# One product with C for two neighbouring units in the recurrent stage of a decoder kernel

## The reference, cut to what matters

```python
def _selective_scan(u, dt, A, Bm, Cm, Dp):
    dA = jnp.exp(dt[..., None] * A)
    dBu = (dt * u)[..., None] * Bm[:, :, None, :]
    def step(h, inp):
        dA_t, dBu_t, C_t = inp
        h = dA_t * h + dBu_t                       # state of 16 per channel
        y = jnp.einsum('ben,bn->be', h, C_t)
        return (h, y)
    ...
    return y + u * Dp

def _mamba(x, in_w, cw, cb, xw, dtw, dtb, A_log, Dp, ow):
    u, z = jnp.split(x @ in_w, 2, axis=-1)         # 512 channels each
    u = jax.nn.silu(causal convolution of u with 4 taps + cb)
    dbl = u @ xw                                   # 64 of dt, 16 of B, 16 of C
    dt = jax.nn.softplus(dbl[..., :64] @ dtw + dtb)
    y = _selective_scan(u, dt, -jnp.exp(A_log), Bm, Cm, Dp)
    return (y * jax.nn.silu(z)) @ ow

for i in range(4):
    x = x + _mamba(layer_norm(x), ...)
```

## Time and profile before

| | |
|---|---|
| median of 3 runs | 4773.03 us |
| profiled execution | 4812.17 us, its span 4810.5 us |
| recurrent stage, first to last scan | 70.95 to 2069 us of the span |
| one of its 16 segments, mean | 125 us |
| VectorE busy over the span | 66%, in the recurrent stage 94% |
| scans: count, mean | 1024, 1251 ns |
| products with C: count, mean | 1024, 675 ns |
| decays: count, mean | 1024, 689 ns |
| drives: count, mean | 1024, 1274 ns |

### The profile page before, as it was taken

One profiled execution on the slowest core, in us unless ns is written; L12 is line 12 of the kernel. 1 busy time (PEld: TensorE's weight loads), 2 busy tenths in 40 slices (PEclk: granted clock), 3 DMA queues, 4 the chain that ended last, 5 costly groups with the idle time before them and its releaser, 6 DMA issues. The chain is left out here.

```text
span 4810.5 us, 50784 instructions
## 1 busy us (share of the span) xinstructions
PE 4110.7 (85%) x16032; PEld 2276.1 (47%) x16032; DVE 3197.0 (66%) x5216; ACT 2001.7 (42%) x3534; POOL 2265.1 (47%) x1928
## 2 busy tenths in 40 slices
PE   7888888888998888759858887999968999966998
PEld 2333333333333333224432336888833444655898
DVE  4999999999999999954466645444445554155433
ACT  5666566656565656432234451111112444222100
POOL 6888888888888888820021112444330111000320
PEclk9999999999999999979768898999977999988899
DMA  4555544554455544510062201000061320000000
GB/s 121 133 134 147 136 139 134 139 140 141 134 136 146 140 133 134 143 43 0 0 122 33 40 11 57 14 26 26 1 155 48 53 52 10 9 16 0 27 20 29
DMA packets 288996, 375.34 MB, mean 78 GB/s; under 512 B 100481, under 2 KB 131516, under 8 KB 288508
## 3 DMA queue, kind: packets, MB, share of 16 engines
q1 hardware_dynamic: 288764, 372.57, 30.4%
HBM read 343.80 MB, written 26.21 MB: 77 GB/s over the span
## 5 line engine op out<-in xcount | busy, mean ns | idle before, releaser
L521 POOL TENSOR_TENSOR arena<-arena 128x512 f32<-128x512 f32 x1024 | 1284.3, 1274 | 260.3 <-DVE psum L764 254.6
L764 DVE TENSOR_TENSOR_SCAN psum<-psum,arena 128x512 f32<-128x512 f32 x1024 | 1280.6, 1251 | 78.7 <-ACT psum L670 78.0
L871 PE MATMUL psum<-arena,base 128*128 128x512 f32 x2048 | 1083.9, 631 | 262.5 <-DVE arena L739 261.5
L670 ACT ACTIVATE psum<-arena 128x512 f32<-128x512 f32 x1024 | 699.5, 689 | 271.5 <-DVE arena L739 252.6
L871 PEld LDWEIGHTS psum<-arena,base 128*128 128x128 f32 x2048 | 348.5, 192 | 921.9 <-DVE arena L739 745.0
L739 DVE TENSOR_TENSOR arena<-psum,arena 128x512 f32<-128x512 f32 x1024 | 691.3, 675 | 0.0
L283 POOL TENSOR_TENSOR rounded<-arena,rounded 128x512 fp32r<-128x512 f32 (+2 forms) x181 | 315.9, 1751 | 791.8 <-DVE rounded L279 791.8
L289 PE MATMUL psum<-rounded 128*128 128x256 f32 (+1 forms) x1728 | 561.6, 325 | 33.1 <-DVE arena L1689 16.2
L290 PE MATMUL psum<-rounded 128*128 128x256 f32 (+1 forms) x1728 | 561.0, 325 | 0.0
L291 PE MATMUL psum<-rounded 128*128 128x256 f32 (+1 forms) x1728 | 560.3, 324 | 0.0
L1158 DVE TENSOR_REDUCE arena<-psum 128x1 f32<-128x512 f32 (+3 forms) x768 | 403.2, 555 | 199.6 <-PE psum L1221 139.1
(11 more groups left out here) (287 smaller groups left out, 5171.7 us busy)
## 6 DMA issues: line engine op xcount, KB each, us to landing
arena<-mb_bc_rows SPq DMA_DIRECT2D x512, 512.0 KB, 4.8
arena<-L_ffn_w SPq DMA_DIRECT2D x34, 512.0 KB, 4.4
arena<-f_parts SPq DMA_DIRECT2D x96, 128.0 KB, 6.5
arena<-l_parts SPq DMA_DIRECT2D x96, 128.0 KB, 6.4
l_v<-arena SPq DMA_DIRECT2D x16, 512.0 KB, 3.6
arena<-l_v SPq DMA_DIRECT2D x32, 256.0 KB, 4.4
f_parts<-arena SPq DMA_DIRECT2D x24, 256.0 KB, 2.4
l_parts<-arena SPq DMA_DIRECT2D x24, 256.0 KB, 2.4
```

The lines of the kernel that those rows point to most:

```text
L521: eng.tensor_tensor(drive[:, u % RD, :], dtu[:, g % 2, m, :], bc_sb[:, v % RB, 0, :], ALU.mult)\
L670: eng.activation(ps[:, DECAY + u % ND, :], dt[:, g % 2, m, :], ACT.Exp, scale=a_neg[:, g // 4 % 2, m, n:n + 1]).then_inc(decay_ready, 1)
L764: eng.tensor_tensor_scan(state(u), state(u), drive[:, u % RD, :], first, ALU.mult, ALU.add).then_inc(scanned, 1)
L871: eng.matmul(ps[:, Y + u % 2, :], sh.ident, hc[:, u % RW, :], start=False, stop=n == NS - 1).then_inc(added_up, 1)
```

## The change

The product with C is made for two neighbouring units (an even u and u+1) at once. The two units' states lie in neighbouring PSUM banks, their products in neighbouring places of the ring, and they share the C row, which is read twice through a broadcast. The pair product stands behind the scan of u+2, so that one scan of the next pair lies between the pair's last scan and its product. Its signal counts two units at once. The two gates that stood ahead of the products of p = 0 and 1 (and 32 and 33) now both stand ahead of the pair product of p = 0 (and 32). The lines from there on move by two or three.

```diff
-        def weigh(u):
-            eng.wait_ge(scanned, u + 1)
+        def weigh_pair(u):
+            eng.wait_ge(scanned, u + 2)
             if u >= RW:
-                eng.wait_ge(added_up, u - RW + 1)
-            eng.tensor_tensor(hc[:, u % RW, :], state(u), bc_sb[:, u // 2 % RB, 1, :], ALU.mult).then_inc(weighted, 1)
+                eng.wait_ge(added_up, u - RW + 2)
+            at, r = DECAY + u % ND, u % RW
+            c_rows = bc_sb[:, u // 2 % RB, 1, :].unsqueeze(1).to_broadcast([P, 2, BANK])
+            eng.tensor_tensor(hc[:, r:r + 2, :], ps[:, at:at + 2, :], c_rows, ALU.mult).then_inc(weighted, 2)
 
-        def gate_before(u):
+        def gates_before(u):
             at = u - HALF
-            if at >= 0 and u % HALF < 2:
-                gate(at // UNITS, at % UNITS // HALF, u % HALF)
+            if at >= 0 and u % HALF == 0:
+                for q in range(2):
+                    gate(at // UNITS, at % UNITS // HALF, q)
...
             eng.tensor_tensor_scan(state(u), state(u), drive[:, u % RD, :], first,
                                    ALU.mult, ALU.add).then_inc(scanned, 1)
-            if u:
-                if u >= HALF + 1 and (u - 1) % HALF < 2:
-                    gate_before(u - 1)
-                weigh(u - 1)
+            if u and u % 2 == 0:
+                gates_before(u - 2)
+                weigh_pair(u - 2)
...
-        weigh(SEGS * UNITS - 1)
+        weigh_pair(SEGS * UNITS - 2)
```

## The result

The changed kernel took 5089.44 us (median; 5088.41 to 5093.23), against 4777.48 us of the kernel before beside it: 1.0657 times as long, interval 1.0627 to 1.0687, 312 us more. The prediction said 5008, range 4900 to 5100, slower with a chance of 0.94. The profiled execution has a span of 5091.5 us. Times and ratios are those of runs in the chip's fast state; a run of split (5690.97 us) and one of the kernel before (10143.09) are in the slow one and not counted.

What follows compares the result with a forecast made beforehand. The prediction took VectorE's ordered list plus its waits to bound the recurrent stage. Added wait of 255 us less 20 us saved work made +235, giving 5008 us, range 4900 to 5100.

Steps and rivals of the forecast that it cites:

- forecast as sized: Whole kernel: added waits less saved work make +235 us, time between 4930 and 5060; chance 0.73.
- the clock's rival: TensorE's clock falls behind new idle pieces, delaying three chains per segment by 1.7 us each: 77 us more, 5085; chance 0.10.
- scans 4, 6: At p = 3 and 5, ScalarE's normalized rows make the next even decay 2.2 us late each: +4.4 per segment.
- additions at 8, 10: VectorE's additions of the last segment's output wait for TensorE's output products: 1.36 and 1.14 us, +1.8 per segment.
- scans 27, 37: At p = 26 and 36, ScalarE's table loads and Silu delay decays: 2.55 and 2.5 us, +4.3 per segment.
- both gates at 34: Gates ahead of the pair product wait for the sum over unit 31, among two convolutions: 4.5 us, +2.5 per segment.
- scan 44: At p = 43, the rows of dt, B and C make decay 44 late: +2.4 us per segment, nothing before.
- The saved instruction: 1024 products of 512 columns become 512 of 1024, saving 0.04 us a pair: 20 us (25 lost to 56 saved).
- The rival of the larger saving: Each pair saves 0.11 us, 56 us in all, and the lead suffices: faster, 4717; chance 0.03.
- The lost lead: Decay ring of four banks: even units keep 1.04 us of lead, before 3.35; added waits 255 us.
- sum per segment: Added waits: 18.0 us in an even segment, 15.6 in an odd one, mean 17, times 15 segment transitions: 255 us.
- Covering for each other: Rival: a wait at one place lets TensorE and ScalarE catch up, taking off 85 us: 4923; chance 0.11.

Runs made afterwards that it cites:

- split: The changed kernel with its pair product written as two products of 512 columns, same place in VectorE's list, each with its own signal: 4994.46 us, 1.044.
- jobs: The changed kernel with three of ScalarE's tasks for the next segment one place later (p = 4, 6 and 44): 4975.72 us, 1.0416.
- near: The changed kernel with the pair product directly behind its own second scan, no scan of the next pair in between: 4900.09 us, 1.0245.
- warm: The changed kernel with three dummy TensorE products of 512 columns at each of p = 3, 35 and 61: 5071.11 us, 1.0606.
- after: The changed kernel itself, with the pair product of 1024 columns, against the kernel before: 5089.44 us, 1.0657.

## Why the prediction came out as it did

The direction and the mechanism were right, and the time lay near the upper end of the range: +235 forecast, +312 measured. It lies outside the forecast as sized (4930 to 5060, chance 0.73) and 4 us from the time of the clock's rival (5085, chance 0.10); the range holds it because it was drawn to take that rival in. Delays in one even segment, in steps, from the starts in its timeline:

| place | forecast | measured after |
|---|---|---|
| scans 4, 6 | 2.2, 2.2 | 2.2, 2.2 |
| additions at 8, 10 | 1.36, 1.14 | 3.1, 1.2 |
| scans 13, 17 | as before, 1.85 | 1.7, 1.7 |
| scans 27, 37 | 2.55, 2.5 | 2.7, 2.5 |
| both gates at 34 | 4.5 | 4.5 |
| scan 44 | 2.4 | 4.6 |
| scan 56 | 0.84 | 0.83 |
| scan 63 | 3.6 | 3.65 |
| second gate at 2 | not priced | 0.8 |

- **The saved instruction** was sized at 0.04 us a pair by the step; it is 0.08 in the even segments (3.36 against 3.44) and some 0.06 in the odd ones. Over the stage 18 us of work went by the recorded waits, forecast 20; it is some 30 if each wait is counted from the step, as there are 123 waits more that each read 0.09 too short. The rival of the larger saving needed 0.11 a pair and a lead that suffices, and the waits refute it. By the Trainium skill, "VectorE: DVE Perf Modes" (The TRN2 errata), the saving would be 80 us, an estimate; its advice of larger tiles holds here in direction and not in size (18 to 30 us).
- **The lost lead**: ten of the twelve prices for an even segment hold within 0.2 us. (Two figures of the prediction are slightly off as worked out there: 5.2 against 0.6 + 3.40 makes the second addition 1.2 late and not 1.14, and the chain of the earlier trace rows is 1.5 times its window and not nearly twice.) jobs and near show the mechanism by itself, and split shows that it is the place in the list.
- **The mis-sized term** is the sum per segment. 17 us were forecast and some 22 measured (323 / 15): 302, 76 and 57 us of waits for decays, gates and additions, where the prediction looked for 280, 65 and 35. The two places of the table that are far off, the first addition and scan 44, and the second gate at p = 2, are those where TensorE worked behind an idle piece at a lower clock: 1.7, 2.2 and 0.8 us in the even segment, some 3 in the odd one (there at 2, 6 and 8, and in two of them at 44). That is about 4 us per segment, 61 us; the rest, under 1 us, is spread over odd segments priced a little low and small waits as the one before scan 50, which I hadn't priced. The rival had named this with three places and 77 us and had got a chance of 0.10; it should have been in the main sum, since the row for it was there and the added waits are themselves what makes TensorE idle (its sums waited 519 us for VectorE's products, before 262). Its price of 1.7 us a place does not follow from that row: 0.74 on average is about half of the 4 us at the lower level, so 1.0 us lost. That its total came so close is in part luck. By the Trainium skill, "TensorE: Matmul & The Clock Gate" (Why this matters for your kernels), idle gaps between bursts are to be avoided for that reason; the rows above agree (3.17 us idle, then 0.77 of the clock).
- **Covering for each other** didn't happen: scan 6 waits as long as scan 4.
- **No other limit appeared.** GpSimd's busy time is the same, 1711.31 against 1715.11 us, over a longer stage.

What stays open: how much the clock costs in the whole kernel, as the dummies moved one of its falls, and three of warm's four executions lost some 16 us that its trace doesn't show.

## What to carry to other kernels

Before two operations on ring buffers are made one, count for each producer the time from the release of its buffer to its next use, in steps of the consumer's list. A pair released together leaves the even member of a ring of four one scan of lead where it had two scans and two products, and each job that the producer does between may then show in full. Where a job must stay, its place relative to the pair's parity is worth more than the instruction saved: moving jobs won 249 us here, the wide product's shorter step 18 to 30.

## What the runs showed of the hardware

- A record's length is not its cost: products of 512 columns read 675 ns and step 590, those of 1024 read 1206 and step 1120, scans read 1.22 us and step 1.13. A product that waits for the scan just ahead of it starts 0.10 us behind that scan's end and not 0.09 ahead (near), so a dependence on the neighbour costs 0.2 us.
- With dummies in front, a stretch keeps the full clock (1.00 against 0.77), and a later stretch, at full clock before the dummies were put in, is granted 0.58 (warm). So work put in at one place can move a fall of the clock to another.
- The same place of the same lists runs at different clocks in one execution: the output products of two odd segments of after at 1.00 and at 0.66, and the addition behind them waits 1.19 and 2.88 us.
